# Gathering x1 rows instead of h1 rows, ScalarE makes h1, and a quarter of the last stage on ScalarE and TensorE

## The reference, cut to what matters

```
x1 = x + layer0(...)                          # 6250 x 512
h  = relu((x1 - mean) / sqrt(var + eps))      # row by row, "h1"
xn = batchnorm(h)                             # over the nodes
agg[n] = mean over edges (s -> n) of xn[s]    # 100000 rows gathered
conv = relu(agg @ W_conv + b_conv)
attn = performer attention of the first 256 nodes of h
y    = conv + attn + h
out  = x1 + batchnorm(y)                      # over the nodes
```

## Time and profile before

| | us |
|---|---|
| three runs | 2971.27, 2972.5, 2979.11; median 2972.5 |
| the profiled execution, own time | 2977.88 |
| its span in the trace | 2975.6 |

### The profile page before, as it was taken

How to read it: one execution, slowest core, us unless ns; L and a number is a source line. 1 busy time by engine, 2 the same in 40 slices (tenths; PEclk the granted TensorE clock), 3 DMA queues, 4 the chain that set the end, 5 groups by cost and what they waited for, 6 DMA issues and landing times. The chain is left out here.

```text
span 2975.6 us, 45964 instructions
## 1 busy us (share of the span) xinstructions
PE 2506.6 (84%) x10691; PEld 1550.3 (52%) x10692; DVE 2155.4 (72%) x3787; ACT 993.1 (33%) x3078; POOL 1852.3 (62%) x1883
## 2 busy tenths in 40 slices
PE   5888728999999999999988798888888889999990
PEld 3555416777777777777766743333333333334440
DVE  8999988898898889889889554444444444445668
ACT  5833335555555555555553610000000000002220
POOL 0000036777777777777749377777777777774658
PEclk7999858999999999999998899999999999999995
DMA  6110047888888888888858877777777777774227
GB/s 208 52 41 37 35 133 220 241 245 246 243 242 247 244 238 245 246 241 243 246 191 271 283 211 210 211 210 210 210 210 210 210 209 210 209 210 124 67 56 296
DMA packets 243452, 588.30 MB, mean 198 GB/s; under 512 B 57744, under 2 KB 82832, under 8 KB 243400
## 3 DMA queue, kind: packets, MB, share of 16 engines
q0 software_dynamic: 133120, 443.52, 51.2%
q1 hardware_dynamic: 110280, 144.14, 14.7%
HBM read 533.43 MB, written 54.10 MB: 197 GB/s over the span
## 5 line engine op out<-in xcount | busy, mean ns | idle before, releaser
L506 POOL DMA_INDIRECT big<-feat_table,idx x880 | 837.0, 951 | 687.5 <-ACT idx L531 409.5
L1146 POOL DMA_INDIRECT big<-h_table,idx x784 | 741.2, 945 | 252.9 <-issue 233.1
L801 PE MATMUL psA<-big,onehot 128*128 128x260 f32 x1760 | 440.2, 393 | 15.9 <-DVE big L683 13.8
L801 PE MATMUL psB<-big,onehot 128*128 128x260 f32 x1760 | 433.4, 389 | 7.3
L557 ACT ACTIVATE big<-big,late_weights 128x65 f32<-128x65 f32 x1760 | 434.0, 340 | 0.0
L801 PEld LDWEIGHTS psA<-big,onehot 128*128 128x128 f32 x1760 | 317.8, 190 | 100.7 <-issue 37.0
L801 PEld LDWEIGHTS psB<-big,onehot 128*128 128x128 f32 x1760 | 317.0, 190 | 64.0 <-DVE acc L693 17.6
L531 ACT CAST idx<-minorB 128x8 int32 (+1 forms) x101 | 20.3, 203 | 942.3 <-DMA big<-h_table,idx 942.3
L1568 DVE TENSOR_TENSOR acc<-acc,psA 128x512 f32 x180 | 123.3, 685 | 216.1 <-PE psA L1912 216.1
L1568 DVE TENSOR_TENSOR acc<-acc,psCD 128x512 f32 x180 | 123.2, 685 | 212.3 <-PE psCD L1912 210.5
L1911 PE MATMUL psCD<-big,onehot 128*128 x360 | 189.7, 609 | 44.9 <-ACTq L1299 42.9
(11 more groups left out here) (450 smaller groups left out, 3742.5 us busy)
## 6 DMA issues: line engine op xcount, KB each, us to landing
nodes_all<-slot_nodes SPq DMA_DIRECT2D x56, 512.0 KB, 5.7
big<-feat_table,idx POOLq DMA_INDIRECT x880, 3.8
feat_table<-big SPq DMA_DIRECT2D x49, 264.0 KB, 2.1
x_table<-acc SPq DMA_DIRECT2D x49, 256.0 KB, 3.8
h_table<-big SPq DMA_DIRECT2D x49, 256.0 KB, 3.8
big<-h_table,idx POOLq DMA_INDIRECT x784, 3.7
big<-h_table SPq DMA_DIRECT2D x49, 256.0 KB, 2.6
big<-x_table SPq DMA_DIRECT2D x49, 256.0 KB, 4.1
```

The lines of the kernel that those rows point to most:

```text
L506: g.indirect_dma_start(ring[:, b.k, q * SB + u, :], None, feat_table, bass.IndirectOffsetOnAxis(ap=idx[:, 2 * b.k + q, u:u + 1], axis=0)). ...
L801: ins = pet.matmul(psum[:, 512 * hf:512 * hf + HALF_W], onehot[:, q, u % SB, :], ring[:, b.k, u, HALF_W * hf:HALF_W * (hf + 1)], start=(u ...
L1146: g.indirect_dma_start(big[:, place:place + D], None, h1_table, bass.IndirectOffsetOnAxis(ap=idx[:, r.c % CHUNK_CYCLE, b:b + 1], axis=0)). ...
```

## The change

1. `h1_table` and its 49 stores go. `x1_table` rows become `ROW1_W` = 514 floats (2056 bytes): the 512 of x1, then the row's scale and bias, which `group_rstd` copies behind each row in `acc`. SP stores x1 by groups of tiles, once a group's scale and bias are there. `h1_tile` no longer waits for a store.
2. The gathers read `x1_table` rows of 514 floats. After each group of four has arrived, ScalarE runs a Relu with scale and bias in place on each of the four chunks, and only then signals `arrived`.
3. In the dense stage `h_in` gets x1 rows, and ScalarE makes h1 of them (`make_h`). `make_y` waits for that.
4. 35 instead of 14 x1 tiles are loaded ahead of the last stage: 14 where they were, 13 after the last `h_in` load, 8 after the last y.
5. In the last stage every fourth tile (12 of 49) leaves VectorE and GpSimd. TensorE transposes y, ScalarE applies scale and shift per partition, TensorE adds x1 (a matmul with the identity) and transposes back by four matmuls, ScalarE copies the sum to `obuf`.

```diff
+ROW1_W = D + 2
-        h1_table = nc.dram_tensor("h1_table", (TILES * P, D), F32).ap()
+        x1_table = nc.dram_tensor("x1_table", (TILES * P, ROW1_W), F32).ap()
...
+        def x1_store_slot(n):
+            return min(TILES - 1, GROUPS[n][1] + 3)
...
                 sp.wait_ge(x1_ready, t + 1)
-                sp.dma_start(x1_table[t * P:(t + 1) * P, :], acc[:, t, 0:D]).then_inc(
-                    x1_stored[sum(t >= end for end in CLEARED[1:])], 16)
...
+                for n, (first, end) in enumerate(GROUPS):
+                    if x1_store_slot(n) == t:
+                        sp.wait_ge(rstd1_ready, n + 1)
+                        for u in range(first, end):
+                            store_x1(u)
...
-                        g.indirect_dma_start(big[:, place:place + D], None, h1_table,
+                        g.indirect_dma_start(big[:, place:place + ROW1_W], None, x1_table,
...
             if t >= KEPT:
-                    act.wait_ge(h1_stored[q], 16 * (t // KEPT))
                     act.wait_ge(grams, t - KEPT + 1)
...
                     act.wait_ge(h_arrived[group], r.turn(64, 64 + arrived_before[group]))
-                    act.sem_inc(arrived, 1)
+                    for b in range(4 * u, 4 * u + 4):
+                        place = places[(r.c * SB + b) % RING1]
+                        row, factors = big[:, place:place + D], big[:, place + D:place + ROW1_W]
+                        ins = s.activation(row, row, ACT.Relu, scale=factors[:, 0:1], bias=factors[:, 1:2])
+                    ins.then_inc(arrived, 1)
...
+            def make_h(t, q, loads):
+                act.wait_ge(hc_in[q], loads)
+                s.activation(h_in[:, q, :], h_in[:, q, :], ACT.Relu, scale=ln[:, 0, bass.ds(t, 1)],
+                             bias=ln[:, 1, bass.ds(t, 1)]).then_inc(h_made, 1)
...
                     turn_out(i * 2 + (q + 1), 1 - q)
                     keep_y(i * 2 + q, q)
+                    make_h(i * 2 + (q + 1), 1 - q, i * 16 + (16 + 16 * q))
...
+            def normalize_columns(n):
+                act.wait_ge(yT_ps, ONCE + n + 1)
...
+                for k in range(KD):
+                    ins = s.activation(yT[:, n % 2, k * P:(k + 1) * P], yT_of[n % 2][:, k * P:(k + 1) * P], ACT.Identity,
+                                       scale=scale2[:, k:k + 1], bias=shift2[:, k:k + 1])
+                ins.then_inc(yT_ready, 1)
+            def keep_out(n):
+                act.wait_ge(turned_back, ONCE + n + 1)
+                if n >= 1:
+                    act.wait_ge(out_stored[3], 16 * n)
+                s.copy(obuf[:, 3, :], back_of[n % 2]).then_inc(turned_out, 1)
...
-                v.scalar_tensor_tensor(stat[:, 1, of], mean1[:, of], -0.5, stat[:, 3, of], ALU.mult, ALU.mult).then_inc(rstd1_ready, 1)
+                link(v.scalar_tensor_tensor(ln[:, 1, of], mean1[:, of], -0.5, ln[:, 0, of], ALU.mult, ALU.mult))
+                v.tensor_copy(acc[:, of, D:ROW1_W], ln[:, :, of].rearrange("p u t -> p t u")).then_inc(rstd1_ready, 1)
...
+            def turn_back(n):
+                t = 4 * n + 3
+                wait_x1(pe, t)
+                if n >= 2:
+                    pe.wait_ge(turned_out, ONCE + n - 1)
+                pet.matmul(back_of[n % 2], ident, x1_places[t % AHEAD], start=True, stop=False)
+                pe.wait_ge(yT_ready, ONCE + n + 1)
+                for k in range(KD):
+                    ins = pet.matmul(back_of[n % 2][:, k * P:(k + 1) * P], yT[:, n % 2, k * P:(k + 1) * P], ident,
+                                     start=False, stop=(k == KD - 1))
+                ins.then_inc(turned_back, 1)
```

More of the change, by code:

```diff
@@ L401, in build @@
         KEPT = 6
-        h1_stored = [sem(f"h1_stored{q}") for q in range(KEPT)]
+        h_made = sem("h_made")
         den_ready = sem("den_ready")
@@ L468, in layer0_sync, with store_x1 @@
             sp.dma_start(xlast[0:LAST, :], x[(TILES - 1) * P:N, :]).then_inc(x_last, 16)
[L470 to L473, removed]
+            def store_x1(t):
+                sp.dma_start(x1_table[t * P:(t + 1) * P, :], acc[:, t, 0:ROW1_W]).then_inc(
+                    x1_stored[sum(t >= end for end in CLEARED[1:])], 16)
             for u in range(2):
@@ L929, in build @@
         STEP_AT = SB + SB // 2
-        places = list(range(0, SB * D + SB // 2 * D, D)) + [SB * D + SB // 2 * D + 6 * D + n * D for n in range(SB + 4)]
-        assert places == [D * n + (6 * D if n >= STEP_AT else 0) for n in range(RING1)] and CHUNK_CYCLE * SB == RING1
-        assert places[STEP_AT + SB] == SB * D + SB // 2 * D + AD_W
+        places = [ROW1_W * n + (6 * D if n >= STEP_AT else 0) for n in range(RING1)]
+        assert places[STEP_AT] == AD_AT + 6 * D and places[-1] + ROW1_W == KEYS_AT + 2 * COLS + GAP
+        assert CHUNK_CYCLE * SB == RING1
         class Row:
@@ L1051, in build, with places_of @@
         bn2_sd = sem("bn2_sd")
[L1052 to L1057, removed]
+        def places_of(*areas):
+            return [area[:, n * D:(n + 1) * D] for area in areas for n in range(area.shape[1] // D)]
@@ new lines, in build @@
+        x1_places = x1_first + x1_second + x1_third
+        SECOND, AHEAD = len(x1_first) + len(x1_second), len(x1_places)
+        assert AHEAD + len(x1_first) >= TILES
+        reused_in = [sem(f"x1_in{n}") for n in range(len(x1_first) - 6)] + [rows_loaded, masks_in] + x_in
+        reused_from = [0] * (len(x1_first) - 6) + [16 * (BATCHES + 1), MASKS_16 * (BATCHES + 1) // 2] + [16 * QUADS] * 4
+        later_in = [(x1_stored[n], 16 * (CLEARED[n + 1] - CLEARED[n])) for n in range(3)] + [
+            (x_loaded[n], 48 if n == 2 else 16) for n in range(3)] + [(feat_stored[n], 16 * (DENSE_PAIRS + 1 - n)) for n in range(2)]
@@ new lines, in build, with x1_signal, wait_x1 @@
+        LATER_SIZES = (3, 3, 3, 2, 2, 3, 3, 2)
+        assert sum(LATER_SIZES[0:5]) == len(x1_second) and sum(LATER_SIZES[5:]) == len(x1_third)
+        later_group = [n for n, size in enumerate(LATER_SIZES) for _ in range(size)]
+        def x1_signal(t):
+            place = t % AHEAD
+            return reused_in[place] if place < len(x1_first) else later_in[later_group[place - len(x1_first)]][0]
+        def wait_x1(engine, t):
+            place = t % AHEAD
+            if place < len(x1_first):
+                engine.wait_ge(reused_in[place], reused_from[place] + 16 * (t // AHEAD + 1))
+            else:
+                n = later_group[place - len(x1_first)]
+                engine.wait_ge(later_in[n][0], later_in[n][1] + 16 * LATER_SIZES[n])
@@ L1073, in row_of, with wait_x1_stored @@
             return vector.rearrange("(u c) -> u c", u=1)
-        def wait_h1_stored(engine):
-            for q in range(KEPT):
-                engine.wait_ge(h1_stored[q], 16 * len(range(q, TILES, KEPT)))
+        def wait_x1_stored(engine):
+            for n in range(3):
+                engine.wait_ge(x1_stored[n], 16 * (CLEARED[n + 1] - CLEARED[n]))
         def layer1_sync(sp):
-            wait_h1_stored(sp)
             sp.wait_ge(grams, TILES)
@@ L1172, in layer1_gpsimd @@
                     pool.sem_inc(hold, 1)
-            for t in range(TILES):
+            for n, t in enumerate(t for t in range(TILES) if t % 4 < 3):
                 q = t % 4
-                pool.wait_ge(shifted, t + 1)
-                pool.wait_ge(x1_in[t % AHEAD], x1_in_from[t % AHEAD] + 16 * (t // AHEAD + 1))
+                pool.wait_ge(shifted, n + 1)
+                wait_x1(pool, t)
                 if t >= 4:
@@ L1188, in make_h1 @@
                     row = row.rearrange("p (k c) -> p k c", k=KD)
-                return s.activation(target, row, ACT.Relu, scale=stat[:, 3, t:t + 1], bias=stat[:, 1, t:t + 1])
+                return s.activation(target, row, ACT.Relu, scale=ln[:, 0, t:t + 1], bias=ln[:, 1, t:t + 1])
             def deviations(n):
@@ L1323, in layer1_scalar @@
             keep_y(1, 1, True)
+            make_h(2, 0, 32)
             with act.Fori(1, DENSE_PAIRS) as i:
@@ L1330, in layer1_scalar @@
             s.activation(sd2, var2, ACT.Sqrt, bias=small[:, 0:1]).then_inc(bn2_sd, 1)
+            def normalize_columns(n):
+                act.wait_ge(yT_ps, ONCE + n + 1)
+                if n == 0:
+                    act.wait_ge(diag2_ready, 2 * KD)
+                if n >= 2:
+                    act.wait_ge(turned_back, ONCE + n - 1)
+                for k in range(KD):
[7 more added lines that the diff above has]
+                s.copy(obuf[:, 3, :], back_of[n % 2]).then_inc(turned_out, 1)
+            normalize_columns(0)
+            for n in range(QUADS):
+                if n + 1 < QUADS:
+                    normalize_columns(n + 1)
+                keep_out(n)
         def layer1_vector(dve, link, links):
@@ L1614, in average, with make_y @@
                                 rdeg[:, bass.ds(t, 1)], None, ALU.mult).then_inc(aggn_ready, 1)
-            def make_y(t, q, loads, first=False):
+            def make_y(t, q, first=False):
```

(12 more changed lines are left out.)

99 lines of the change are left out of this document (62 added, 37 removed).

## The result

The changed kernel takes 3002.2 us (median of 4, 3000.7 to 3005.2) where the kernel before, in runs beside it, takes 2973.8 (2971.3 to 2979.1): 1.0087 times as long, 95% interval 1.0075 to 1.0099. It is slower by three times what a measurement tells from no change. The forecast, 2974.5 in 2960 to 2985, was wrong.

A forecast was written before the change was run, and what follows sets the result against it. It took GpSimd's gathers (980 us), TensorE in the dense stage, and VectorE, GpSimd and full DMA engines in the last stage as limits. Terms -8 + 0.5 + 3.0 + 15 - 8.5 = +2.0 us gave 2974.5 us, range 2960 to 2985.

The forecast's parts named there:

- A: h1 stage without stores of h1: waits for them go, first gather comes earlier, -8 us (bounds -2.4 and -14.3).
- the ring of four x tiles covers four of VectorE's 1.3 us turns: h1 stage: x loads moved past SP's bursts of eight x1 stores, some 4 us, stay covered by four buffers.
- the gathers start 4 us later: h1 stage: the price named if the x tile buffers did not cover SP's store bursts, 4 us.
- 0.2 us in each of seven others: h1 stage: cost of the added small operation in each `group_rstd` after the first, beside a TensorE that never stops.
- The end of TensorE's long idle time: h1 stage: removing ScalarE's wait at 1648 lets TensorE's idle 7.16 us end 2.4 us earlier.
- The wait of 3.88 us: h1 stage: TensorE's wait at 1681.33, `group_rstd` sitting behind a ScalarE waiting for stores, goes: 3.88 us.
- B: Gathers: still 1.25 us each with 2056-byte rows; Relus on ScalarE add +0.5 at the start, +3.0 at the end.
- C: Dense stage: the new Relu delays ScalarE's copy and the next convolve, 0.66 us per pair of tiles, +15 us.
- Rival 1: Dense stage: the Relu finds room in idle ScalarE, costing 0 to +4, total 2961 us; chance 0.20.
- D: Loads ahead: 21 of 35 leave the last stage's full DMA engines for an idle stretch, gating nothing there.
- E: Last stage: VectorE keeps 37 tiles, output buffers limit the first part, adds 53.9 us from 62.7: -8.5 us.
- rival 3: h1 stage: x1's last stores or SP's bursts replace the removed waits, gain 0, total 2982.5 us; chance 0.08.

The follow-up runs named there:

- e6: Changed kernel with memsets held until the chain on the places ends and factors copied by scalar_tensor_tensor, stores of x1 still in bursts: 2988.7 us, ratio 1.0040.
- e5: e3 with the two factors put beside x1 by scalar_tensor_tensor where it was a tensor_copy: 2978.0 us, ratio 1.000.
- e2: Changed kernel with stores of x1 issued one per slot of SyncE, not eight at once: 2998.6 us, ratio 1.0071.
- e1: Changed kernel with GpSimd's two memsets held until VectorE has ended its chain on the places: 3000.7 us, ratio 1.0080.
- e3: Changed kernel with both edits, stores of x1 one per slot and memsets held until the chain ends: 2991.7 us, ratio 1.0056.
- e7: e5 and e4 together, against the changed kernel: 2960.1 us, ratio 0.9934.
- e12: Kernel before, with the chain on the places moved behind x1 tile 42 and memsets held until it has ended: 2974.1 us, ratio 0.9985.
- e9: e7 with the last stage's adds as before, all 49 tiles on VectorE and GpSimd, loads ahead kept: 2970.7 us, ratio 0.9973.
- e11: e7 without the four Relus per gathered group on ScalarE, only the count passed on: 2959.0 us.
- e4: Changed kernel with the dense stage's Relu of tile t+1 moved behind the copy of tile t+2 on ScalarE: 2986.9 us, ratio 1.0039.
- e10: e7 with 14 loads of x1 ahead of the last stage instead of 35, the quarter kept: 2969.6 us, ratio 0.9968.

## Why the prediction was wrong

*A failed, by 25 us.* The step that failed is "the ring of four x tiles covers four of VectorE's 1.3 us turns", with its price for lost cover, "the gathers start 4 us later". It set this cover, 5.2 us, against SyncE's issue time of a burst alone (some 4 us; 5.13 measured), and left out that the load's own landing has to fit into the same cover. In the trace the cover is 5.5 us, the late issue takes 4.05 of it, the landing 6.5, and VectorE waits 5.02. Its four waits for x sum to 11.9 us in the changed kernel, and bursts cost 10 to 13 us of the stage by themselves (e6 against e5 and the runs with the same stage).

The other part was not in the prediction at all: an instruction of VectorE that is held by GpSimd's memset. Between e6 and the changed kernel, which differ in the meetings and the kind of the copy (142.2 and 157.15), it is 15 us. The 0.45 us between chain and memset stood in the trace of before, and I priced the new copy by its own duration, "0.2 us in each of seven others", without asking what GpSimd does beside it. The late x load also moved the chain into the memset (in e2, without bursts, they don't meet), so the two causes are linked: e1 against e3, 6.4 us, is what the bursts cost where the copy is held anyway.

What the theory said of the stores of h1 was borne out in the main: with the bursts and the held copy gone the stage is 129.5 to 131.8 us, 8 to 10 under before, where -8 was forecast. The traces show its parts. The end of TensorE's long idle time, forecast 2.4 us earlier, comes 3.2 us earlier in e5 and 0.9 in e7 (98.70 us after the first x1 in the kernel before). The wait of 3.88 us is gone in both, and the granted clock in the last stretch is 1.00 where it was 0.87. From that idle time to the first gather it is 34.1 us in e5 for 41.3 before, 7.2 less, where 3.88 and 2.5 were forecast. No run takes the stores of h1 away and nothing else, and in e12, which keeps them, that wait is 1.6 us and the stage 137.4; how much of the 8 to 10 is the stores' alone stays open.

*B, gathers.* Borne out. 1.25 us each, share 0.76. From first to last gather it is 0.3 and 0.5 us more than before in e7 and e5, 2.2 in the changed kernel, and 2.7 in e9, whose gathers are those of e7: the 1.7 above the forecast are no more than one execution differs from another. The end: +3.2, e11 gives 3.0 to the Relus.

*C, dense.* The mechanism was right, the size 15 against 12.2: two tiles took 8.45 us where 8.54 was forecast, and over the whole stage less. That it follows from order alone, e4 shows: 192.0. That this is 2.3 under the stage of before was not looked into. Rival 1 (the Relu finds room) therefore described a kernel in which one instruction stands elsewhere.

*D and E.* -7.8 against -8.5; the statement that the loads gate nothing and show in E is what e10 measured.

The range ended at rival 3 with A at 0. It took the stage of before as the worst case for a change that removes waits, and rival 3, which named SP's bursts, let them take back no more than the gain; no bound stood for a stage longer than before.

## What to carry to other kernels

Before adding or shifting a copy or tensor_scalar between SBUF tiles on VectorE, look at what GpSimd runs at that time: its price may be the rest of that instruction. Use another form (here scalar_tensor_tensor), hold the memset, or try another engine (not tried here). Spread stores over the slots in which loads with a small ring are issued, and set the issue time of a burst and the landing of the load behind it, together, against the cover of the ring. On an engine with much idle time the place in its order still costs: put new work behind the instruction on which the next engine waits.

## What the runs showed of the hardware

Wherever they met one of the two memsets (12.2 and 5.3 us), VectorE's TENSOR_SCALAR and COPY between SBUF tiles, otherwise 0.2 to 0.4 us long, took as long as the memset had left: TENSOR_SCALAR 11.63 and 12.47 us in the first and 1.77 to 4.04 in the second, COPY 9.46 to 9.82 and 4.04 to 5.16. They ended 0.02 to 0.28 us behind the memset. With nothing held ahead of them, scalar_tensor_tensor (0.16 to 0.69), bn_stats (0.69), a reciprocal between SBUF tiles (0.17 to 0.19) and a copy out of PSUM (0.28, at 1665.69 in e5) passed the same memsets. The amount of data does not decide it: 16 numbers a partition wait as 440 do.
